# Recurrent block on one Trainium2 core: the attention loop's scores, row maxima and projections in another order inside each step of two slots

## The reference

```python
x  = L0_attn_x
xn = layernorm(x)
s  = linear attention, 16 heads of 8, gated, then a 4-expert feed-forward   # layer 0
g  = silu(top-1 of 16 experts, capacity limited)
x  = x + s * g
xn = layernorm(x)                                                           # layer 1
q, k, v = einsum('bsx,xAnh->Abnsh', xn, w);  q = q + q_bias      # 16 heads of 64
a  = q k^T / 8 + relative_causal(q emb^T / 8)                    # positions by sinusoids
a  = softmax(where(tril, a, -1e9))
s  = (a v) @ out_kernel + out_bias
g  = silu(sigmoid(xr W_r) * (relu(xk W_k)^2 W_v))                # xr, xk: mix with the token before
x  = x + s * g
```

## Time and profile before

| | before |
|---|---|
| median of 3 runs | 1278.44 us |
| the profiled execution's own time | 1278.44 us |
| its span in the trace | 1276.5 us |
| PE busy | 1172.4 us, 92% |
| POOL busy | 825.1 us, 65% |
| DVE busy | 814.1 us, 64% |
| ACT busy | 681.2 us, 53% |

### The profile page before, as it was taken

The page is one execution under the profiler, slowest core; times in us unless marked ns, Lnnn a source line. Parts: engine busy times, 40 slices in busy tenths (PEclk is TensorE's granted clock), DMA queues, the critical chain, the costliest instruction groups (busy, mean ns, idle before and its releaser), DMA issues.

```text
span 1276.5 us, 31138 instructions
## 1 busy us (share of the span) xinstructions
PE 1172.4 (92%) x11813; PEld 765.5 (60%) x11820; DVE 814.1 (64%) x2017; ACT 681.2 (53%) x1375; POOL 825.1 (65%) x1098
## 2 busy tenths in 40 slices
PE   4899678998985879999999999999999999999997
PEld 2344555667662546766666676676666676667665
DVE  3777356732546458669658757767866866875652
ACT  2533152235422437656656665665665665666665
POOL 1777200040502578887888878878888788888996
PEclk9998688999986889999999999999999999999998
DMA  8200200011301330230121103103013013011101
GB/s 328 90 1 1 74 1 1 1 34 54 96 1 36 76 95 6 44 80 15 43 60 35 43 19 76 43 18 76 20 25 85 11 43 76 19 43 42 37 2 34
DMA packets 74752, 60.09 MB, mean 47 GB/s; under 512 B 38950, under 2 KB 69162, under 8 KB 73516
## 3 DMA queue, kind: packets, MB, share of 16 engines
q1 hardware_dynamic: 73580, 56.02, 17.0%
q0 software_dynamic: 1024, 2.09, 0.6%
HBM read 19.70 MB, written 4.72 MB: 19 GB/s over the span
## 4 chain that ended last, share of the span: by engine, by line
PE 61%; POOL 4%; DVE 1%; ACT 1%; DMA 1%; issue 1%; SPq 1%; POOLq 0%; DVEq 0%
PE S L1711 9%; PE S L1712 9%; PE S L1713 9%; PE A L1701 8%; PE O L1725 5%; PE O L1723 5%; PE O L1726 5%; PE M L1692 2%; POOL plow L1446 2%; PE M L1669 2%; PE M L1671 2%; PE M L1670 2%; PE M L1684 1%; POOL pair_w L1576 1%; PE M L1675 1%
## 5 line engine op out<-in xcount | busy, mean ns | idle before, releaser
L1446 POOL TENSOR_TENSOR plow<-prob 128x512 f16<-128x512 f32 (+3 forms) x640 | 593.9, 938 | 122.5 <-ACT prob L1919 99.1
L1919 ACT ACTIVATE prob<-S,keep_sigma 128x512 f32<-128x512 f32 (+3 forms) x640 | 395.7, 625 | 281.9 <-PE S L1713 279.8
L2018 DVE CUSTOM_DVE_ANT_0 junk<-A,mask_rows,part 128x512 bf16<-128x512 f32 (+3 forms) x384 | 248.8, 648 | 115.2 <-PE A L1701 98.4
L1723 PE MATMUL O<-V,prob 128*128 128x65 f16 x2176 | 234.2, 193 | 9.1 <-POOL plow L1446 9.1
L1701 PE MATMUL A<-rows 96*128 96x512 f16 (+3 forms) x640 | 222.1, 348 | 13.6 <-DVE part L2015 7.3
L1725 PE MATMUL O<-V,prob 128*128 128x64 f16 x2176 | 233.9, 195 | 0.0
L1726 PE MATMUL O<-V,plow 128*128 128x65 f16 x2176 | 233.0, 192 | 0.0
L1723 PEld LDWEIGHTS O<-V,prob 128*128 128x128 bf16 x2176 | 203.3, 97 | 36.1 <-issue 7.5
L1711 PE MATMUL S<-rows 97*128 97x512 f16 (+3 forms) x640 | 224.0, 350 | 0.4 <-ACT kvs L1891 0.2
L1712 PE MATMUL S<-rows 96*128 96x512 f16 (+3 forms) x640 | 223.0, 348 | 0.0
L1713 PE MATMUL S<-rows 96*128 96x512 f16 (+3 forms) x640 | 221.3, 346 | 0.0
(11 more groups left out here) (342 smaller groups left out, 1884.3 us busy)
## 6 DMA issues: line engine op xcount, KB each, us to landing
rows<-stage_rows SPq DMA_DIRECT2D x64, 256.0 KB, 3.2
V<-stage_v SPq DMA_DIRECT2D x16, 516.0 KB, 4.4
W<-in_W SPq DMA_DIRECT2D x2, 2048.0 KB
shifted<-turned SPq DMA_DIRECT2D x32, 128.0 KB, 2.2
rows<-stage_pos SPq DMA_DIRECT2D x64, 64.0 KB, 2.8
w<-in_w SPq DMA_DIRECT2D x2, 1024.0 KB
xe_rows<-zero SPq DMA_DIRECT2D x1, 1280.0 KB, 9.3
ye_rows<-xe SPq DMA_DIRECT2D x5, 256.0 KB, 3.1
```

Of the source, the lines that this page charges most:

```text
L1446: pool.tensor_tensor(plow[:, k % PB, 0:w], full, full.bitcast(BF16).rearrange("p (q e) -> p q e", e=2)[:, :, 1], ALU.subtract).then_inc(s_ ...
L1723: pe.matmul(both, high[:, cs, 1], vh[h][:, j, 0:HS + 1], start=(j == 0 and s == 0), stop=False, skip_group_check=True)
L1919: act.activation(prob[:, k % PB, 0:w], S[k % 2][:, 0:w], ACT.Exp, scale=sigma[:, 2 * p + h:2 * p + h + 1]).then_inc(s_exp, 1)
L2018: dve.tensor_tensor_reduce(junk[:, g % 2, 0:w], A[g % 2][:, 0:w], add, -1.0, before, ALU.add, ALU.min, out).then_inc(s_max, 1)
```

## The change

On PE both score tiles of a step come first, then A and the items of the first slot, then A and the items of the second, then the values as before. On ACT and DVE the items of an even slot are handled in the odd slot after it, behind the exponentials (ACT) or the row maxima (DVE) of both. Nothing is added or taken away; POOL's and SP's programs are the same.

```diff
@@ tensor program
                 for k in two:
                     if k < ALL:
                         score_tile(*divmod(k, SLOTS))
+                for k in two:
+                    if k < ALL:
                         row_tile(*divmod(k, SLOTS))
                         slot_items(*divmod(k, SLOTS))
@@ scalar program
                 if n < ALL:
                     exps(*divmod(n, SLOTS))
                     p, at = divmod(n, SLOTS)
-                    for (kind, rel, c, tok) in plan[p == PAIRS - 1][at]:
-                        item(kind, rel, c, tok, p, 0)
+                    if at % 2:
+                        for (kind, rel, c, tok) in plan[p == PAIRS - 1][at - 1] + plan[p == PAIRS - 1][at]:
+                            item(kind, rel, c, tok, p, 0)
@@ vector program
                     high = high if at else 0
-                    for (kind, rel, c, tok) in plan[last][at]:
-                        item(kind, rel, c, tok, p, high)
-                        high += kind in ("q", "k", "v")
+                    if at % 2:
+                        for (kind, rel, c, tok) in plan[last][at - 1] + plan[last][at]:
+                            item(kind, rel, c, tok, p, high)
+                            high += kind in ("q", "k", "v")
```

## The result

| | before | after |
|---|---|---|
| median, 6 runs each | 1278.16 us (1276.20 to 1281.77) | 1287.02 us (1280.75 to 1288.64) |
| ratio of the means, 95% interval | | 1.0055 (1.0028 to 1.0083): 3.6 to 10.6 us more |
| profiled execution, span | 1278.44, 1276.5 us | 1283.69, 1281.8 us |

A forecast was written before the change was run, and what follows sets the result against it. The prediction took PE's streaming of columns to bound the attention loop. Its terms, -1.1 (slot 51) + 0.8 (slot 22) + 0 (pair starts) = -0.3 us, took 1278.44 us to 1278.1, range 1275.5 to 1283.0.

The forecast's parts named there:

- A of slot 3: Pair start: would wait an estimated 0.2 us for slot 1's maxima, covered because V of slot 0 has 0.90 us to spare.
- a join behind a split's start: DVE beside POOL: could lose up to a split (1.04 us), 7 x 0.5 = 3.5 us more than the sum, giving 1281.6.
- the join of slot 17: DVE join step that took 1.20 us beside a split; the split would move ahead of it, so no loss counted.
- Slot 51: PE's 0.16 us stall before A, waiting for slot 49's maxima, would go in seven pairs: 1.1 us gained.
- Slot 22: PE's k item would wait 0.12 us for the bank of slot 20's q item: seven pairs, 0.8 us (0.8 to 3.0).
- Pair starts: PE's waits for POOL at six pair starts, 9.6 us in all, would stay: 0 us gained.
- my own signs: Forecast wrong if a pair is over 0.5 us longer, PE awaits DVE at A (slots 11-34), or slot 0's V waits under 0.5.
- A: Rival: in slots 11 to 34 DVE falls behind, slower by 5.2 us, 1283.6 us; chance 0.15.
- B: Rival: six pair starts shrink with POOL earlier; 9.6 us and slot 51's 1.1 go, 1267.7 us; chance 0.08, full or half.

The follow-up runs named there:

- third experiment: The changed kernel, but with ACT scaling the outputs behind both slots' exponentials and not between them: 1278.82 us, ratio 1.0000 to the kernel before.
- first experiment: The kernel before with only PE's order new, ACT and DVE as before the change: 1302.31 us, ratio 1.0183 to the kernel before.
- the fourth: The changed kernel with DVE's old order, an even item's low part ahead of the odd slot's maxima: 1318.82 us, ratio 1.0314 to the kernel before.

## Why the prediction was wrong

**The step that failed.** "Every pair of producer and consumer on PE is two slots apart (S for its bank, A for its bank), and both ends move together, so in a full step the distance stays." Both ends do move, but what lies between them changes. Between S of an odd slot and S of the next odd slot lay the items of the next step's even slot, and now lie those of its own step. Where only the next step has one, the distance shrinks by an item: from 2.58 to 1.90 us at slots 47 and 49. I had checked this for items and their banks, there with the widths of S alone, and not for S and its exponentials. ACT needed 2.34 us at slot 47, because the scaled outputs run between the two exponentials; with them last 1.91 us do (third experiment). Seven times 0.44 us were missed, 3.1 us.

For A the sentence fails in another way. DVE takes the maxima of an even and an odd slot one after the other, and A of the even slot now comes later by S of the odd one, so both maxima end later, while A of the next odd slot stands where it stood. A of slot 3 was worked out so in the prediction; A of slots 17, 43 and 51 in the last pair was not.

**What I left out.** I counted seven pairs and not the last, which has its own items. It lost 1.95 us; in steps 8, 60 and 72 for the same reason as at slot 49, as the third experiment shows by 0.00 there. In steps 16, 42 and 50, 0.1 to 0.2 us each stay with every kernel that has PE's new order. There A of the odd slot starts 0.07 us after the end of the maxima of two slots before, as here at slot 43, where it could have started at 1227.87:

```profile
1227.24 0.75 DVE L2021 CUSTOM_DVE_ANT_0 junk<-A,mask_rows,part 128x512 bf16<-128x512 f32 x1 [0.17 <-DVE part L2018]
...
1228.06 0.23 PE L1701 MATMUL A<-rows 96*128 96x128 f16 x1
```

This is read from the trace; no kernel was made to test it.

**The cast.** I said that a join behind a split's start could lose a split. It did, in two pairs of seven, 1.02 us each. I had followed the join of slot 17, which the change did free, and not the other eleven. The cast of slot 13 went the other way: 1.19 us in the trace before and 0.41 after. The prediction had a price for such a loss, 3.5 us in all, and left it out of the sum.

**What held.** Slot 51: 1.2 us gained for 1.1 forecast. Slot 22: 0.19 us a pair for 0.12, in the given bounds, and by the chain that was named. Pair starts unchanged, with the estimated 0.2 us of A of slot 3 inside the wait. By my own signs, a pair longer by over 0.5 us meant wrong: it is 0.50 in the plain pairs and 1.52 in two, and in those two PE did wait for DVE at A.

**The rivals.** A had the sign and about the size (1283.6 us), but not the mechanism: DVE was busy 27.65 of 33.00 us in slots 11 to 34, less than before, and in five pairs of seven PE never waited for it at A. The main wait is for ACT in slot 49, outside A's place. A grain of it is true: the maxima come later at A of slots 3, 17, 43 and 51. B, the pair starts, was rightly held unlikely for this change; the time itself is real. Since A had 0.15 and the true mechanism none, the range ended at 1283.0, 4.0 us below the result.

## What to carry to other kernels

When the order inside a software-pipelined step changes, work out for every double-buffered bank what lies on the producer between a use and the next use, with the items of this step and of the next, and hold it against what the consumer's queue does between the same two points: equal distances in slots are not equal distances in time. On the consumer, put what frees a bank ahead of what nobody waits for. And where PE is the bound, compare starts step by step in the two traces, the last round included: a stall shorter than a matmul's listed length is in no list of waits.

## What the runs showed of the hardware

- The loop repeats from execution to execution: behind slot 8 of the first pair, a step of the same kernel differs by 0.02 us or less from pair to pair, apart from the collisions and a few longer steps (step 32 in one pair of the first experiment, 0.6 us, steps 32 and 34 in two pairs of the fourth, 2.9 us, and step 38 in one pair with the memset ahead, 0.08 us; why wasn't looked into). The work ahead of it doesn't repeat: it was 5.5 us shorter to 4.1 us longer than in the profile of before. In the profiled executions these two differences make up the whole time within 0.8 us. The timed runs have no such split, but their spread is of that size, so that the timed ratio and the loop's own difference agree only to a few us.
- Who comes first by hundredths of a microsecond decides which of VectorE and GpSimd is held: the cast 0.03 us behind the split took 1.29 us instead of 0.41; at the same time stamp the split took 1.31 instead of 1.04.
- Once two of them collide, the one that is held ends at nearly the same time, whatever the overlap: a cast that started 0.03 to 0.79 us behind a split ended 1.32 us after the split's start in all 60 places, and a split that started up to 0.24 us behind a cast, or with it, ended 1.30 to 1.32 us after the cast's start (1.16 us long behind slot 19's cast in the trace before, 1.29 with the outputs last, 1.31 with the reduction ahead). The exception is the cast behind a memset.
